# A graph kernel whose scatter hops wait through ScalarE: one wait a step on TensorE, 32-bit step tables, and VectorE's wait for its own last sum moved ahead of the one-hot or the weighting

## What is computed

```python
# block 0: three graph convolutions
for i in range(3):
    h = h * out_norm[:, None]
    h = segment_sum(h[src], dst)          # gather rows, add them up by target node
    h = h * in_norm[:, None]
    h = h @ W[i] + b[i]                   # relu after the first two
# block 1: two graph attentions with 4 heads of 64 features, self loops added
h = x @ W
alpha = leaky_relu(a_src[src] + a_dst[dst])
e = exp(alpha - segment_max(alpha, dst)[dst])
out = segment_sum(e / segment_sum(e, dst)[dst] * h[src], dst) + bias
```

## Time and profile before

| | |
|---|---|
| median of 3 runs | 6875.43 us (6857.97 to 6877.12) |
| the profiled execution | 6875.32 us, span 6873.5 us |
| busy: PE / DVE / ACT / POOL | 61% / 53% / 31% / 60% |
| granted TensorE clock, mean | 0.71 |
| instructions | 84355 |

### The profile page before, as it was taken

The page is one execution under the profiler, slowest core; times in us unless marked ns, Lnnn a source line. Parts: engine busy times, 40 slices in busy tenths (PEclk is TensorE's granted clock), DMA queues, the critical chain, the costliest instruction groups (busy, mean ns, idle before and its releaser), DMA issues. The chain is left out here.

```text
span 6873.5 us, 84355 instructions
## 1 busy us (share of the span) xinstructions
PE 4202.8 (61%) x14997; PEld 2812.5 (41%) x14997; DVE 3621.6 (53%) x12180; ACT 2136.3 (31%) x7094; POOL 4130.3 (60%) x4276
## 2 busy tenths in 40 slices
PE   8555555565555556555555636666666556666774
PEld 7333333343333334333333424444444334444442
DVE  6444444544444444444444636666666556666667
ACT  4000000020000002000000247677777467767774
POOL 7666666366666664666666356566664556666663
PEclk7666666776666668666666867777778777777776
DMA  3333333133333332333333233333333323333334
GB/s 100 95 95 89 91 91 91 55 103 90 91 89 91 90 90 85 90 91 90 91 91 90 85 112 88 87 90 89 88 90 86 104 77 89 88 89 87 89 89 133
DMA packets 309602, 625.46 MB, mean 91 GB/s; under 512 B 85343, under 2 KB 180411, under 8 KB 309080
## 3 DMA queue, kind: packets, MB, share of 16 engines
q0 software_dynamic: 192928, 530.18, 27.7%
q1 hardware_dynamic: 109800, 88.51, 4.1%
q10 hardware_dynamic: 6384, 1.39, 0.1%
HBM read 573.23 MB, written 47.33 MB: 90 GB/s over the span
## 5 line engine op out<-in xcount | busy, mean ns | idle before, releaser
L1127 PE MATMUL main<-ring,oh 128*128 x4992 | 2039.7, 573 | 1582.9 <-DVE oh L1413 775.2
L695 POOL DMA_INDIRECT ring<-conv_tab,csrc x2346 | 2221.4, 947 | 1232.7 <-issue 613.0
L1421 DVE TENSOR_TENSOR acc<-acc,main 128x264 f32 (+2 forms) x4160 | 1762.7, 424 | 1964.9 <-PE main L1127 688.1
L1127 PEld LDWEIGHTS main<-ring,oh 128*128 128x128 f32 x4992 | 1337.3, 286 | 2282.1 <-issue 2038.2
L707 POOL DMA_INDIRECT ring<-attn_tab,sidx x1664 | 1586.1, 953 | 1079.4 <-issue 441.2
L1230 PE MATMUL main<-ring,oh 128*128 128x264 f32 x3328 | 1367.9, 528 | 354.8 <-ACT ring L959 190.5
L1413 DVE TENSOR_SCALAR oh<-iota,dloc 128x128 f32<-128x128 f32 x2505 | 765.0, 306 | 474.1 <-issue 327.2
L959 ACT ACTIVATE ring<-ring 128x64 f32<-128x64 f32 x3328 | 906.5, 340 | 0.0
L1230 PEld LDWEIGHTS main<-ring,oh 128*128 128x128 f32 x3328 | 672.9, 247 | 546.0 <-issue 349.0
L937 ACT ACTIVATE oh<-iota,dloc 128x128 f32<-128x128 f32 x1664 | 527.2, 391 | 2.7 <-DMA attn_tab<-oh 2.7
L1766 DVE TENSOR_TENSOR ring<-ring 128x128 f32<-128x128 f32 x1664 | 463.6, 284 | 0.0
(11 more groups left out here) (215 smaller groups left out, 3012.1 us busy)
## 6 DMA issues: line engine op xcount, KB each, us to landing
ring<-conv_tab,csrc POOLq DMA_INDIRECT x2346
ring<-attn_tab,sidx POOLq DMA_INDIRECT x1664
ring<-attn_tab SPq DMA_DIRECT2D x14, 896.0 KB, 8.2
conv_tab<-oh SPq DMA_DIRECT2D x12, 896.0 KB, 4.0
flag_room<-start_rows SPq DMA_DIRECT2D x416, 8.0 KB
flag_room<-end_rows SPq DMA_DIRECT2D x416, 8.0 KB
x_tab<-acc SPq DMA_DIRECT2D x7, 896.0 KB
oh<-x_tab SPq DMA_DIRECT2D x7, 896.0 KB
```

Source lines behind the costliest of these rows:

```text
L695: pool.indirect_dma_start(ring3[:, c % U, 0:C], None, conv_tab[k], bass.IndirectOffsetOnAxis(ap=csrc[:, c:c + 1], axis=0)).then_inc(gather ...
L1127: nc.tensor.matmul(main[s % 4][:, 0:width], oh[:, (s % OHR) * P:(s % OHR + 1) * P], ring[:, bass.ds(slots[s % 8], width)], start=True, sto ...
L1421: nc.vector.tensor_tensor(a, a, main[k][:, 0:width], ALU.add).then_inc(added, 1)
```

## The change

- `step_words` and `step_tab` hold 32-bit values and three rows only; ARRIVALS moves to a table of its own (`arrival_tab`, 16-bit). One more copy out of PSUM on DVE and two more small DMAs on SP in the preparation.
- ACT gets `relay_steps(k)` in each hop: every four steps a load of four ARRIVALS, and in each step a wait for the one-hot, a wait for the arrival, and an increment of `step_ready`. The key and flag DMAs of hop 0 are put between these steps (`neighbour_keys`).
- PE waits for `step_ready` alone, and loads SLOT_AT alone.
- DVE's wait for its own last sum now stands ahead of the one-hot, in place of the wait for product s-1; ahead of the sum only the wait for the product is left. In attention the wait for the last sum stands ahead of the weighting (`settled`), in each step.

The diff, cut to its core:

```diff
@@ step_values
         def step_values(engine, row, s, n):
 
             return nc.values_load_multi_w_load_instructions(
-                step_tab[row:row + 1, s:s + n], engines=[engine], min_val=1 if row == ARRIVALS else 0, max_val=LAST_AT[row],
-                skip_runtime_bounds_check_because="chunk, slot and tile are clamped on the chip")[1]
+                step_tab[row - 1:row, s:s + n], engines=[engine], min_val=0, max_val=LAST_AT[row],
+                skip_runtime_bounds_check_because="slot and tile are clamped on the chip")[1]
+
+        def arrivals_of(engine, s):
+
+            return nc.values_load_multi_w_load_instructions(
+                arrival_tab[0:1, s:s + 4], engines=[engine], min_val=1, max_val=EC,
+                skip_runtime_bounds_check_because="chunk counts are clamped on the chip")[1]
@@ SyncE, preparation
-            sp.dma_start(step_words.rearrange("w (b p) -> (w b) p", p=P), step_rowsT).then_inc(words_in, 16)
-            sp.wait_ge(words_in, 16)
+            sp.dma_start(arrival_words.rearrange("w (b p) -> (w b) p", p=P), arrival_rowsT).then_inc(words_in, 16)
+            sp.dma_start(step_words.rearrange("w (b p) -> (w b) p", p=P), step_rowsT[SB:4 * SB, :]).then_inc(words_in, 16)
+            sp.wait_ge(words_in, 32)
+            sp.dma_start(arrival_tab, arrival_words).then_inc(words_in, 16)
             sp.dma_start(step_tab, step_words).then_inc(words_in, 16)
@@ ScalarE
-            act.wait_ge(keys_ready, 1)
...
-                act.wait_ge(flags_out, 64)
+            def neighbour_keys(s):
...
+                    if s == SROW_AT:
+                        act.wait_ge(keys_ready, 1)
...
+                    if s == SROW_AT + 8:
+                        act.wait_ge(key_out, 16)
...
+                    if s == EROW_AT + 56:
+                        act.wait_ge(flags_ready, 1)
...
+                    if s == S - 1:
+                        act.wait_ge(key_out, 112)
+            def relay_steps(k):
+
+                if k == 0:
+                    act.wait_ge(words_in, 64)
+                    act.nop(nofuse=True)
+                for s in range(S):
+                    if s % 4 == 0:
+                        counts = arrivals_of(mybir.EngineType.Activation, s)
+                    act.wait_ge(onehots, oh_base(k) + s + 1)
+                    act.wait_ge(arrived[k], counts[s % 4])
+                    act.sem_inc(step_ready, 1)
+                    if k == 0:
+                        neighbour_keys(s)
@@ TensorE, conv
                     if s % 8 == 0:
-                        counts = step_values(mybir.EngineType.PE, ARRIVALS, s, 8)
                         slots = step_values(mybir.EngineType.PE, SLOT_AT, s, 8)
-                    pe.wait_ge(onehots, oh_base(k) + s + 1)
-                    pe.wait_ge(added, k * S + s + 1)
-
-                    pe.wait_ge(arrived[k], counts[s % 8])
-                    pe.nop(nofuse=True)
+                    pe.wait_ge(step_ready, k * S + s + 1)
@@ VectorE
             nc.vector.tensor_scalar(col[SLOT_AT], col[SLOT_AT], float(AW), None, ALU.mult).then_inc(words_ready, 1)
             hist(3, 4)
             dve.wait_ge(words_T, 1)
+            link(nc.vector.tensor_copy(arrival_rowsT, psb[0:SB, P:2 * P]))
             nc.vector.tensor_copy(step_rowsT, psb[0:4 * SB, P:2 * P]).then_inc(words_ready, 1)
@@ VectorE, accumulate and conv
             def accumulate(at, k, width, s):
 
-                dve.wait_ge(products_done, CR + s + 1)
-                dve.wait_ge(added, 4 + s)
                 a = acc[:, bass.ds(at, width)]
...
-                    dve.wait_ge(products_done, CR + k * S + s)
+                    dve.wait_ge(added, 4 + k * S + s)
                     onehot(bass.ds(s + AHEAD, 1), (s + AHEAD) % OHR)
+                    dve.wait_ge(products_done, CR + k * S + s + 1)
                     accumulate(sums_at[s % 8], s % 4, C + 1 if k == 0 else C, k * S + s)
@@ VectorE, attention
+                        def settled(k):
+                            dve.wait_ge(added, 4 + s0 + k)
+
                         def add(k):
+                            dve.wait_ge(products_done, CR + s0 + k + 1)
                             accumulate(sums_at[k], k % 4, AW, s0 + k)
 
                         rescaled = rescale()
                         for k in range(G):
+                            settled(k)
                             if k == G - LEAD:
                                 add(k)
```

More of the change, by code:

```diff
@@ L98, in gnn @@
         end_any = dram("end_any", (1, SX))
-        step_words = dram("step_words", (4, SX), U16)
+        arrival_words = dram("arrival_words", (1, SX), U16)
+        step_words = dram("step_words", (3, SX), I32)
         conv_tab = [dram(f"conv_tab{k}", (NT * P, C)) for k in range(HOPS)]
@@ L290, in gnn @@
         flags_ready = sem("flags_ready")
-        flags_out = sem("flags_out")
+        step_ready = sem("step_ready")
         words_T = sem("words_T")
@@ L802, in _ @@
             copy_projected(NT - 1)
-            act.wait_ge(keys_ready, 1)
[L805 to L808, removed]
+            def neighbour_keys(s):
                 kv = keys[0:1, 0:SX * P].rearrange("o (b p e) -> (o p) b e", p=P, e=P)
-                nc.scalar.dma_start(key[:, :, 0:1], kv[:, :, 0:1]).then_inc(key_out, 16)
@@ L811, in _ @@
                 kn = keys[0:1, 2:SX * P + 2].rearrange("o (b p e) -> (o p) b e", p=P, e=P)
[L812 to L816, removed]
@@ L817, in _ @@
-                nc.scalar.dma_start(end_any.rearrange("o (b p) -> (o p) b", p=P), eany).then_inc(flags_out, 16)
-                act.wait_ge(flags_out, 64)
+                with nc.allow_non_contiguous_dma(reason="one element of each step"):
+                    if s == SROW_AT:
+                        act.wait_ge(keys_ready, 1)
+                        nc.scalar.dma_start(keys[0:1, 1:1 + SX * P].rearrange("o (b p e) -> (o p) b e", p=P, e=P),
+                                            key[:, :, 1:P + 1]).then_inc(key_out, 16)
+                    if s == SROW_AT + 8:
+                        act.wait_ge(key_out, 16)
+                        nc.scalar.dma_start(key[:, :, 0:1], kv[:, :, 0:1]).then_inc(key_out, 16)
+                        nc.scalar.dma_start(key[:, :, P + 1:P + 2], kn[:, :, P - 1:P]).then_inc(key_out, 16)
+                    if s == EROW_AT + 56:
+                        act.wait_ge(flags_ready, 1)
+                        nc.scalar.dma_start(start_rows.rearrange("(b p) e -> p b e", p=P), b3(sfr)).then_inc(key_out, 16)
+                        nc.scalar.dma_start(end_rows.rearrange("(b p) e -> p b e", p=P), b3(efr)).then_inc(key_out, 16)
+                        nc.scalar.dma_start(start_any.rearrange("o (b p) -> (o p) b", p=P), sany).then_inc(key_out, 16)
+                        nc.scalar.dma_start(end_any.rearrange("o (b p) -> (o p) b", p=P), eany).then_inc(key_out, 16)
+                    if s == S - 1:
+                        act.wait_ge(key_out, 112)
@@ L874, in rectify_centred @@
                                      ).then_inc(nb_ready, 1)
+            relay_steps(2)
             rectify_centred(0)
@@ L1369, in _ @@
                 scale_rows(q)
-            dve.wait_ge(words_in, 32)
+            dve.wait_ge(words_in, 64)
             dve.wait_ge(rowsT_read, KB)
```

10 lines of the change are left out of this document (7 added, 3 removed).

## The result

The kernel after takes **6694.7 us** (median of four, 6688.9 to 6700.9) against 6871.9 us (median of four) for the kernel before: a ratio of 0.9745, 95% interval 0.9728 to 0.9763. That is 177 us less. The forecast was 6350 us, 525 us less; its range, 6200 to 6700 us, holds the result by 5 us, at the end that belongs to rival 1 and not to the forecast. Two later comparisons gave 0.9744 (0.9727 to 0.9760) and 0.9751 (0.9735 to 0.9768).

A forecast was written before the change was run, and what follows sets the result against it. PE and DVE, with PE's recurring stops, were taken to set the hops' pace, not the gathers. From 6875.3 us, hops -587 and attention +55 gave 6343, stated as 6350 us; range 6200 to 6700 us.

The forecast's parts named there:

- rival 1: PE's stops go with steps or time, not instructions: 59 stay, 1086 to 1117 us a hop, 6600 to 6700 us; chance 0.17.
- TensorE's sequencer itself crawls: In the hops' stops PE's waits and register operations last up to 1.4 us against medians of 51 and 37 ns.
- if a stop comes every 101.5 instructions, it comes every 19.8 steps: 42 stops, 42 x 6.4 = 269 us a hop: PE in the hops: 41 instead of 58 instructions a group cut stops from 59 to 42, 2.6 us a group instead of 3.64.
- one about every 8: In attention, stops counted over some 250 steps, taken as some 95 PE instructions apart, near the hops' 101.5.
- 32-bit loads, "taken as the same": Register loads from the 32-bit tables were to take today's time, with half and double as bounds; no row showed one.
- rival 3: 32-bit loads at half the time: hops at gather pace, 188 us less at 104 group turns, 6100 us; chance 0.08.
- Group of eight after, 7.1 us: Hop group without stops: 4.7 for seven plain steps, about 0.3 for low clock, 2.1 for the turn; 9.7 with stops.
- plain sum, 0.67 us: DVE's plain step in a hop, sum to sum, with the new order: 0.67 us against 0.62, +0.05.
- Relay at nothing: ACT's relay in the hops: 1.5 to 2.6 us for four steps against 2.7, so it keeps up and costs nothing.
- Order in attention, +55 us: DVE's wait ahead of the weighting lengthens attention steps by 0.04 or 0.12 us; bounds 0 and 108, 55 us taken.
- the row's 0.08 us: DVE in attention: the trace shows the next operation starting before the last ended, 0.08 us an operation against the skill.
- rival 5: ACT's relay sets the hops' pace at 0.9 to 0.97 us a step: groups 11.0 to 11.5 us, 6775 to 6900; chance 0.06.

## Why the prediction was right or wrong

- **What bounds it:** right that neither gathers nor shares but stretches in which TensorE crawls set the hop, and wrong in what they are. "TensorE's sequencer itself crawls" is half of it: its records do stretch, but the work that it has already taken is late too (9.5 us above).
- **The step that failed:** "if a stop comes every 101.5 instructions, it comes every 19.8 steps: 42 stops, 42 x 6.4 = 269 us a hop". They stayed 13 steps apart, 59 in hop 1, and 10.0 us long, and the streams of five instructions a step have 153 to 165 in the three hops where those of seven have 136 to 146 (runs of two or more long gaps). By the forecast's own count, quiet group against mean group, they cost (11.1 - 5.4) x 104 = 593 us a hop where it had found 378. The instruction count was a coincidence of two stages, and partly a miscount: "one about every 8" steps in attention takes in the turns of a group of sixteen. By the rule for long gaps an attention layer of before has 103 runs of them, 8 steps apart, but 65, 12 steps and 18.5 us apart, without the gaps at the turns, and where no stops occur a layer has 50 gaps over 2.4 us, all at turns. What the two stages have in common is that gathers run in both, with stops some 20 us apart (59 in 1200 us of a hop). Rival 1 named this ("stops go with steps or with time"), and its 6600 to 6700 us hold the result; but its quiet group was 6.8 to 7.1 us and its stops 3.64 us a group, where 5.4 and 5.7 were measured, so it is right by two errors against each other, and that the range held the result was luck.
- **32-bit loads, "taken as the same":** a third instead. Both bounds, half and double, missed. It is rival 3, which had the hops at the gathers' pace and 188 us less in attention; the loads went its way and further, and the stops kept the rest: the gap at a group's turn in attention fell from 6.1 to 3.5 us in the mean, but the one ahead of the third sum grew from 0.7 to 3.1 us and that ahead of the eleventh from 0.8 to 2.5 us, and on a chip without stops both are 0.7 us.
- **Group of eight after, 7.1 us:** 5.4 us in the quietest one in twenty, since the turn of 2.1 us all but vanished with the load. The plain sum, 0.67 us, was right (0.66).
- **Relay at nothing:** right. It costs nothing visible (0.67 us a step with it, where no gathers are) and gains 28 to 56 us.
- **Order in attention, +55 us:** wrong in sign. The two layers together get 23 us shorter by it with tables of 32 bits, 31 us with tables of 16. A price of 0.04 to 0.12 us an operation was charged as if VectorE set the pace; why the move gains rather than costs is not shown. The section of the Trainium skill that the prediction sets against its row (VectorE: DVE Perf Modes, The DRAIN you can't avoid) also says that a next operation which is not held starts earlier, so the row's 0.08 us is at odds only with the half that the prediction quotes.
- **The sum:** hops -114 us instead of -587, attention -63 instead of +55, elsewhere -9. In rival 5 the upper end doesn't follow from its terms: groups of 11.5 us give 3588 us for the hops and 6931 us in all, not 6900.

Open: which part of a gather stops TensorE (GpSimd's work, the transfers, writes into the ring), whether TensorE ends its work late or only reports it late, why on some chips only, and whether gathers spaced by 1.4 us would beat 1155 us a hop there. No version was found that beats the kernel after on chips with stops; on the others the gathers' 1.25 us bound all of them.

## What to carry to other kernels

Before pricing a stall per instruction, look for a place where the engine is nearly idle: if others still wait 20 us for twenty of its instructions, where 2.4 us is the usual, the stall isn't its program's. Count it by one rule in every stage and in both kernels, and leave out the gaps that the program makes itself. Then take away whole neighbours, one per stage of the same run, until it goes. A saving on a consumer is worth what its producer's pace leaves: without stops every variant measured is hidden under gathers 1.25 us apart, with them most of the saving goes into the stops (a quiet group 7.9 to 5.4 us, 260 us a hop, of which 36 to 41 us are left). And time the baseline beside every run: here the chip is worth 1250 us, the change 177.

## What the runs showed of the hardware that was not expected

- Registers from a 32-bit table: eight in 0.60 us, sixteen in 1.10 us on VectorE; from a 16-bit table 1.83 and 3.59 us, and four in 0.88 us on ScalarE.
- On some chips gathers by GpSimd 1.25 us apart at the closest, of 1 KB or of 64 bytes a row, go with stops of TensorE of 10 us, some 20 us apart, at a granted clock of 0.50 (half the columns) and of 0.69 in the mean (after); on four other chips a hop with gathers 1.25 us apart shows two at most. Without gathers there are none on either. Within the stops sums follow one another by multiples of 0.70 us, with four, five and seven TensorE instructions a step.
- Without gathers a step runs at 0.67 us with the relay and all loads in it: 557.4 and 557.6 us for 832 steps on two chips.
- After a GpSimd gather a fill of 0.11 us is free, but waiting for one on its own semaphore puts 0.78 us ahead of the next gather instead of 0.19 us.
